# Attention tiles of 8 rows and 16 pixels instead of 4 rows and 32, with x fetched once more for them

## Chip, cores and metric

The kernel runs on one core of a Trainium2 chip. The metric is the device time of one execution in microseconds: the median of the runs.

## What is computed

x has the shape (4, 256, 64, 64), float32. The first layer makes 49 logits for each pixel by a dilated 7x7 convolution and a 1x1 convolution, takes the softmax of them, and uses it to weight the 49 dilated neighbours of the pixel in all 256 channels. The second layer adds a gelu term with a state vector and normalises over the channels.

```python
k = conv(x, w1, padding 6, dilation 2) + b1          # 256 -> 128 channels, 7x7
k = conv(k, w2) + b2                                 # 128 -> 49, 1x1
attn = softmax(k, axis=1)
shifts = [xp[:, :, 2*u:2*u+64, 2*v:2*v+64] for u in range(7) for v in range(7)]
x = einsum('bkchw,bkhw->bchw', shifts, attn)
y = gelu(yc.T[None, :, None, :] + x * D)             # yc: scan over 64 steps
out = layernorm over channels of (x + y), times ln_w, plus ln_b
```

## The kernel before

Because of the dilation, rows and columns of one parity never meet the others. The kernel works in 8 units: batch (4) times the parity of the rows (2). A unit has 32 rows; the two parities of the columns, called w, stay side by side, each 32 pixels wide. The channels are two halves h of 128 partitions.

In each unit `conv(n, ...)` (line 457) computes the logits of unit n on TensorE, in 49 steps of 20 matmuls, from row combinations that GpSimd and VectorE make of the raw rows and that `v_high` (ScalarE) and `v_low` (VectorE) turn into two float16 parts. Between those steps TensorE does the attention of the unit before, m = n - 1. The order on each engine is written out by hand: `unit` on TensorE (line 586), on ScalarE (974), on VectorE (1522), on GpSimd (380). Engines meet by semaphores only, and each queue is served in order.

The attention of a unit goes like this. `turn_logits` transposes the logits, VectorE and ScalarE take the softmax, `turn_attention` transposes back, and ScalarE copies the result to AT (pixels on the free axis, the 49 taps on the partitions, three empty rows above and below). `spread` (516) then builds the band: for the 128 pixels of a tile (4 rows of 32) it selects with a shifted 0/1 matrix `sel`, column by column, the weight with which each input pixel of the tile goes into each output pixel around it. A call covers one of the 10 output rows of all 16 tiles: 32 matmuls of 16 columns into one PSUM bank, which `band_high` (ScalarE, 915) and `band_low` (VectorE, 1484) copy out as two float16 parts. `apply` (530) multiplies x by the band: a call y covers one half of the rows (q), one channel half (h), one column parity (w), and for each tile that reaches these rows three matmuls (high x high, low x high, high x low). The moving side is up to 10 rows of 32 pixels of the band; the weights are the 128 pixels x 128 channels of XT. XT is made by `turn_x` (571), which transposes the tiles' pixels out of the raw rows of the unit, and by `turned_x` (ScalarE, 895) and `turned_x_low` (VectorE, 1387).

After `apply`, `attended` (ScalarE, 920) copies the result to o, VectorE forms the gelu arguments (1492), ScalarE the gelu (930), VectorE the residual (1505), GpSimd the sums of the two channel halves (`sum_rows`, `sum_squares`), TensorE sums over the channels (`mean`, `variance`, 560 and 566), ScalarE spreads the means and takes the inverse deviation, VectorE centres and normalises, ScalarE applies scale and shift, and SP stores. x is loaded by SP into two buffers, raw0 and raw1, one unit ahead.

At the start the weights are combined and split, so unit 0 runs more slowly between that work; the last attention (m = 7) has no convolution beside it, has six PSUM banks for the spreads instead of two, and an order of its own.

## Time and profile before

| | |
|---|---|
| median of 3 runs | 812.79 us (812.68 to 813.52) |
| profiled execution | 813.03 us, of which the span is 810.9 us |
| TensorE busy | 758.2 us (93%), weight loads 448.2 us |
| VectorE busy | 677.6 us (84%) |
| ScalarE busy | 566.1 us (70%) |
| GpSimd busy | 191.0 us (24%) |
| DMA | 41.78 MB, 133598 packets, nearly all under 512 B |

All durations in the text come from the one profiled execution, of which the span is what the profile shows; 2.1 us lie around it. Of the span, 0 to 142 us are the start with unit 0 and the first attention's softmax, then come six like periods of 89.8 us up to 680.5 us, then the last two attentions. In the rows, L544 is line 544 of the kernel; PE is TensorE, PEld its weight loads, DVE VectorE, ACT ScalarE, POOL GpSimd, and ACTq or SPq the sequencer of an engine, where semaphore waits and DMA issues stand.

### The profile page before, as it was taken

The page shows a single profiled execution, that of the slowest core. Times are in us where ns is not written, and L with a number is a line of the kernel's source. Part 1 is how long each engine was busy: PE and PEld are TensorE (multiplying, and loading weights), DVE is VectorE, ACT ScalarE, POOL GpSimd, SP SyncE. Part 2 cuts the span into 40 slices and gives each one's busy share as a digit, 9 for nine tenths or more (in the row PEclk, how much of TensorE's full clock was granted, in tenths as well). Part 3 has the DMA queues.
Part 4 walks back from the last instruction along what each step waited for, and adds up shares of the span by engine and source line. Part 5 has one row for each costly group of instructions (what it writes and reads, how often), then busy time and mean ns, then how long its engine had stood idle before and what let it go on. Part 6 is the DMA issues. An engine that isn't in the chain of part 4 may idle for free.

```text
span 810.9 us, 27182 instructions
## 1 busy us (share of the span) xinstructions
PE 758.2 (93%) x12242; PEld 448.2 (55%) x12242; DVE 677.6 (84%) x867; ACT 566.1 (70%) x917; POOL 191.0 (24%) x102
## 2 busy tenths in 40 slices
PE   4969989999999999999999999999999999997994
PEld 1535545764567545664567545764567455754671
DVE  0898997989888988989888888998888888595765
ACT  2873545768786796678786787678786777568546
POOL 4114113114211341114301431115302421022011
PEclk9979999999999999999999999999999999999988
DMA  9460050001602035201702053201711020201104
GB/s 295 130 105 2 3 93 16 3 1 24 135 4 53 3 77 81 55 2 27 132 2 55 2 107 53 55 2 27 132 27 30 2 53 4 55 2 48 39 22 104
DMA packets 133598, 41.78 MB, mean 52 GB/s; under 512 B 133145, under 2 KB 133226, under 8 KB 133226
## 3 DMA queue, kind: packets, MB, share of 16 engines
q1 hardware_dynamic: 132248, 40.01, 22.2%
q8 instruction: 96, 1.57, 0.8%
q10 hardware_dynamic: 1234, 0.04, 0.1%
q14 instruction: 20, 0.16, 0.1%
HBM read 23.27 MB, written 16.78 MB: 49 GB/s over the span
## 4 chain that ended last, share of the span: by engine, by line
PE 42%; ACT 20%; DVE 17%; issue 5%; POOL 2%; DVEq 0%; ACTq 0%
PE cv L484 20%; PE wk L525 9%; PE wk L544 4%; ACT chs L903 4%; ACT V L860 4%; PE wk L583 3%; POOL chs L371 2%; PE ms L556 2%; DVE o L1507 2%; DVE V L1359 2%; DVE Z L1400 2%; ACT ms L953 1%; DVE XT L1390 1%; DVE chs L1459 1%; DVE o L1520 1%
## 5 line engine op out<-in xcount | busy, mean ns | idle before, releaser
L484 PE MATMUL cv<-V,W 128*32 128x496 f16 (+6 forms) x7840 | 428.2, 374 | 3.6 <-issue 1.9
L484 PEld LDWEIGHTS cv<-V,W 128*32 128x32 f16 (+1 forms) x7840 | 198.8, 96 | 201.4 <-issue 15.3
L860 ACT ACTIVATE V<-R,sc 128x1024 f16<-128x1024 f32 (+1 forms) x88 | 109.6, 1274 | 59.6 <-DVE R L1285 50.7
L346 POOL TENSOR_TENSOR R<-raw 128x1152 f32<-128x1152 f32 x32 | 93.1, 2909 | 205.6 <-DVE V L1359 102.8
L1359 DVE SCALAR_TENSOR_TENSOR V<-R,sc,V 128x1024 f16<-128x1024 f32 (+1 forms) x88 | 115.1, 1328 | 2.6 <-ACT V L860 2.6
L544 PE MATMUL wk<-band,XT 128*128 128x224 f16 (+1 forms) x900 | 97.3, 266 | 0.9
L544 PEld LDWEIGHTS wk<-band,XT 128*128 128x128 f16 x900 | 76.6, 98 | 24.6 <-ACT o L926 6.0
L525 PEld LDWEIGHTS wk<-AT,sel 128*128 128x128 f16 x2368 | 73.5, 100 | 15.0 <-issue 11.0
L525 PE MATMUL wk<-AT,sel 128*128 128x16 f16 x2368 | 77.8, 193 | 0.1
L371 POOL TENSOR_TENSOR chs<-o 128x1024 f32<-128x1024 f32 x14 | 45.1, 3223 | 132.1 <-DVE o L1507 123.1
L1285 DVE SCALAR_TENSOR_TENSOR R<-R 128x1024 f32<-128x1024 f32 (+1 forms) x56 | 70.3, 1287 | 0.0
L926 ACT ACTIVATE o<-wk,sc 128x512 f32<-128x512 f32 x56 | 40.0, 730 | 39.8 <-PE wk L544 39.7
L377 POOL TENSOR_TENSOR chs<-tg 128x1024 f32<-128x1024 f32 x14 | 33.9, 2422 | 120.0 <-ACT tg L939 120.0
L917 ACT CAST band<-wk 128x512 f16<-128x512 f32 x74 | 42.7, 587 | 25.4 <-PE wk L525 25.4
L1486 DVE TENSOR_TENSOR band<-wk,band 128x512 f16<-128x512 f32 x74 | 49.3, 688 | 11.3 <-ACT band L917 10.7
L897 ACT ACTIVATE XT<-wk,sc 128x512 f16<-128x512 f32 x64 | 42.8, 678 | 16.2 <-PE wk L583 15.9
L1390 DVE SCALAR_TENSOR_TENSOR XT<-wk,sc,XT 128x512 f16<-128x512 f32 x64 | 46.4, 745 | 6.6 <-ACT XT L897 6.6
L583 PEld LDWEIGHTS wk<-id,raw 128*128 128x128 f32 x256 | 34.9, 209 | 25.3 <-DVE XT L1390 10.5
L1501 DVE SCALAR_TENSOR_TENSOR tg<-o,dcol,yc 128x1024 f32<-128x1024 f32 x28 | 35.9, 1282 | 15.0 <-ACT o L926 15.0
L1520 DVE TENSOR_TENSOR o<-o,ms 128x1024 f32<-128x1024 f32 x28 | 32.9, 1217 | 15.6 <-ACT ms L956 15.6
L583 PE MATMUL wk<-id,raw 128*128 128x128 f32 x256 | 43.3, 306 | 2.0 <-DVE XT L1390 1.5
L1400 DVE SCALAR_TENSOR_TENSOR Z<-cv,sc,Z 128x512 f32<-128x512 f32 (+1 forms) x56 | 41.1, 746 | 3.2 <-ACT Z L871 1.2
(194 smaller groups left out, 916.9 us busy)
## 6 DMA issues: line engine op xcount, KB each, us to landing
raw<-in_x_dram SPq DMA_DIRECT2D x16, 1024.0 KB, 11.3
out_dram<-o SPq DMA_DIRECT2D x28, 512.0 KB, 4.5
w1raw<-in_L_conv_w_dram SPq DMA_DIRECT2D x2, 3136.0 KB, 16.8
out_dram<-o SPq DMA_DIRECT2D x8, 256.0 KB, 3.9
cm<-in_L_conv_Cmat_dram ACTq DMA_DIRECT2D x1, 32.0 KB, 8.3
dcol<-in_L_conv_D_dram ACTq DMA_DIRECT2D x2, 0.5 KB, 10.2
lnw<-in_L_conv_ln_w_dram ACTq DMA_DIRECT2D x2, 0.5 KB, 7.3
lnb<-in_L_conv_ln_b_dram ACTq DMA_DIRECT2D x2, 0.5 KB, 7.4
```

Of the source, the lines that this page charges most:

```text
L346: nc.gpsimd.tensor_tensor(R[buffer][:, :, :, :], rows_of(par, j + 2), rows_of(par, j), ALU.subtract).then_inc(pool_rows, 1)
L371: nc.gpsimd.tensor_tensor(chs[:, :], o[:, q, 0].rearrange("p r w -> p (r w)"), o[:, q, 1].rearrange("p r w -> p (r w)"), ALU.add).then_inc ...
L484: ins = pe.matmul(to.rearrange("p (w t c) -> p w t c", w=2, c=COLS)[:, :, :, c0:c1], W[:, ws, h * K7 + v, k0:k1], slot(n, a)[:, low, :, t0 ...
L525: ins = pe.matmul(spread_bank(m, r)[:, c * TILES:(c + 1) * TILES].rearrange("p (w j) -> p w j", w=2), sel[:, s, f:f + P], AT[:, :, r:r + 2 ...
L544: ins = pe.matmul(apply_bank(m, y)[:, (r0 - 16 * q) * COLS:(r1 - 16 * q) * COLS], XT[:, xl, 8 * w + j, h, :], band[:, bl, 8 * w + j, r0 - ...
L583: ins = pe.transpose(wk[:, g % 2, c:c + P], rows[:, w:4 * WIDTH:2], id32[:, :])
L860: nc.scalar.activation(v_array(n, a, 0), array(a), ACT.Identity, scale=sc[:, par, 3:4]).then_inc(vhi, 1)
L1285: nc.vector.scalar_tensor_tensor(out=part(*out), in0=part(*a), scalar=factor, in1=part(*b), op0=ALU.mult, op1=ALU.add).then_inc(row_made, 1)
L1359: nc.vector.scalar_tensor_tensor(out=v_flat(n, a, 1), in0=array_flat(a), scalar=sc[:, par, 3:4], in1=v_flat(n, a, 0), op0=ALU.mult, op1=AL ...
L1390: nc.vector.scalar_tensor_tensor(out=low, in0=wk[:, g % 2, :], scalar=sc[:, par, 3:4], in1=high, op0=ALU.mult, op1=ALU.subtract).then_inc( ...
L1400: nc.vector.scalar_tensor_tensor(out=out, in0=summed(n, s, p0, p1), scalar=sc[0:p1 - p0, par, scale:scale + 1], in1=other, op0=ALU.mult, o ...
L1486: nc.vector.tensor_tensor(band[:, 1, :, r, :], spread_bank(m, r).rearrange("p (c t) -> p t c", t=TILES), band[:, 0, :, r, :], ALU.subtract ...
```

## The change

The 128 pixels of a tile are now 8 rows of 16 pixels instead of 4 rows of 32: 4 x 2 tiles for each column parity, 16 in all as before. A tile reaches 14 output rows instead of 10, and 19 columns instead of 32 (16 and 3 beyond one edge; the other edge is that of the picture). The band is stored so: 8 groups of 14 rows, each of 2 x 19 columns. `spread` goes by columns of the tile instead of output rows. Eight calls handle two columns of both tiles each, with 28 matmuls; one call the columns 16 to 18 and -3 (56 matmuls), one the columns -2 and -1 (28 matmuls); the copies of the band take 448 elements, the last 224, instead of 512. `apply` has 18 matmuls a call instead of 15: for each of three tile rows and two tile columns three, over 11, 11 and 3 output rows of 19.

`turn_x` no longer reads the raw rows. A tile's 8 rows of 32 pixels (both column parities) are loaded again from DRAM, two DMAs (one for each h) of 128 KB for each pair of tiles, into three buffers in turn: the two halves of AT (free once the spreads of the unit are done) and a new one, xs. `fetch_rows` on ScalarE issues them, eight times in each unit: three behind the last `band_high`, and one each behind `turned_x` 0 to 4. The first three of unit 0 are issued by SP ahead of the second load of x. `turn_x` waits for its rows. The number and shape of the transposes, and of the copies after them, stay.

In unit 0 the `turn_x` calls stand later between the convolution steps, and `turned_x` 0 and 1 and their low parts on ScalarE and VectorE with them. `sel` has 13 shifted patterns instead of 7 in the same space, so GpSimd writes 26 selections instead of 14; of AT it clears only the six empty rows.

```diff
+TROWS, TCOLS = 8, 16
+XROWS, XTILES = ROWS // TROWS, COLS // TCOLS
+STAGES = XROWS * XTILES
+BROWS = TROWS + 2 * PAD
+BCOLS = TCOLS + PAD
+SPREAD = tuple(((c, None), (c + 1, None)) for c in range(0, TCOLS, 2))
+SPREAD += (((16, 0), (17, 0), (18, 0), (-3, 1)), ((-2, 1), (-1, 1)))
...
 def spread(m, r):
-                for c in range(COLS):
-                    s = c + 1 if c < PAD else c - COLS + 7 if c >= COLS - PAD else 0
-                    f = (BROWS - 1 - r) * COLS + COLS - 1 - c
-                    ins = pe.matmul(spread_bank(m, r)[:, c * TILES:(c + 1) * TILES].rearrange("p (w j) -> p w j", w=2),
-                                    sel[:, s, f:f + P],
-                                    AT[:, :, r:r + 29:4, c], start=True, stop=True)
+                for k, (c, edge) in enumerate(SPREAD[r]):
+                    v = 3 - c if c < PAD else c - 6 if c > TCOLS - PAD - 1 else 0
+                    for row in range(BROWS):
+                        f = v * SEL_STEP + (BROWS - 1 - row) * TCOLS + BCOLS - 1 - c
...
+                            attention = AT[:, :, row:last:TROWS, c:c + TCOLS + 1:TCOLS]
...
+                        ins = pe.matmul(to, sel[:, f:f + P], attention, start=True, stop=True)
 def apply(m, y):
-                for j in range(ROWS // 4):
-                    r0, r1 = max(4 * j - PAD, 16 * q), min(4 * j + 4 + PAD, 16 * q + 16)
+                for j in range(XROWS):
+                    r0, r1 = max(TROWS * j - PAD, 16 * q), min(TROWS * j + TROWS + PAD, 16 * q + 16)
...
+                    for e in range(XTILES):
+                        to = out_rows[:, r0 - 16 * q:r1 - 16 * q, (COLS - BCOLS) * e:(COLS - BCOLS) * e + BCOLS]
+                        for k, (xl, bl) in enumerate(((0, 0), (1, 0), (0, 1))):
+                            ins = pe.matmul(to, XT[:, xl, 2 * (XTILES * j + e) + w, h, :],
+                                            band[:, bl, XROWS * w + j, r0 - TROWS * j + PAD:r1 - TROWS * j + PAD,
+                                                 BCOLS * e:BCOLS * e + BCOLS],
 def turn_x(n, par, g, cold=False):
-                        rows = raw[par][:, h, PAD + 4 * j:PAD + 4 * j + 4, :].rearrange("p r w -> p (r w)")
-                        ins = pe.transpose(wk[:, g % 2, c:c + P], rows[:, w:4 * WIDTH:2], id32[:, :])
+                k = STAGES * n + g
+                pe.wait_ge(xs_in[k % 3], 32 * (k // 3) + 32)
...
+                        rows = stage(k)[:, h].rearrange("p r c -> p (r c)")
+                        ins = pe.transpose(wk[:, g % 2, c:c + P], rows[:, w:2 * P:2], id32[:, :])
...
+            def fetch_rows(n, g):
+                k = STAGES * n + g
+                if g < 3:
+                    act.wait_ge(sel_done, STEPS * n)
+                    act.wait_ge(xt_done, STAGES * n)
+                else:
+                    act.wait_ge(xt_done, k - 2)
+                for h in range(HALVES):
+                    act.dma_start(stage(k)[:, h], tile_rows(n, g, h)).then_inc(xs_in[k % 3], 16)
```

## Rows read from the trace of the kernel before

**Rows 1.** Busy time, one steady unit: length, each engine; clock, DMA share, GB/s.

```profile
231.30:321.08 89.78, 87.86 (x1504) 52.47 (x1508) 78.93 (x96) 68.22 (x111) 23.39 (x9) 1.00 0.24 49
```

**Rows 2.** TensorE's timeline: start, duration, instructions merged, idle before and its releaser.

```profile
281.00 1.08 PE L556 MATMUL ms<-chs,ones 128*64 128x512 f32 x4 [0.40 <-POOL chs L377]
...
289.03 1.08 PE L556 MATMUL ms<-chs,ones 128*64 128x512 f32 x4 [1.03 <-DVE o L1520]
```

**Rows 3.** Chain that ended last, 233 to 271 us: start, duration, engine, target, line.

```profile
233.44 2.04 PE wk L525 x64
...
250.39 3.22 PE cv L484 x60
253.61 3.15 PE wk L544 x30
...
256.88 0.02 ACTq L866
...
257.40 0.95 ACT V L860
...
263.95 2.37 DVE o L1507 x2
...
266.39 3.35 POOL chs L371
...
269.79 1.08 PE ms L556 x4
```

**Rows 4.** ScalarE's timeline, 250 to 283 us.

```profile
250.42 0.59 ACT L917 CAST band<-wk 128x512 f16<-128x512 f32 x1 [0.40 <-PE wk L525]
255.33 0.73 ACT L926 ACTIVATE o<-wk,sc 128x512 f32<-128x512 f32 x1 [4.32 <-PE wk L544]
...
280.15 0.69 ACT L897 ACTIVATE XT<-wk,sc 128x512 f16<-128x512 f32 x1 [1.74 <-PE wk L583]
280.86 1.28 ACT L948 ACT_TABLE_LOAD   x1
282.16 0.66 ACT L948 ACTIVATE ms<-ms,eps 128x512 f32<-128x512 f32 x1
```

**Rows 5.** DMA issues: two of ScalarE's sequencer; lines 309 and 303 with landing.

```profile
2.11 1.50 ACTq L1065 DMA_DIRECT2D dcol<-in_L_conv_D_dram  x2
...
6.68 0.96 ACTq L1073 DMA_DIRECT2D lnb<-in_L_conv_ln_b_dram  x2
...
L309 SPq DMA_DIRECT2D out_dram<-o x28: 372/372/1875, 199.6 to 768.4; - x28
...
DMA to landing us min/median/max: 3.8/4.5/6.3
...
L303 SPq DMA_DIRECT2D raw<-in_x_dram x14: 540/3075/6227, 44.9 to 571.0; - x14
...
DMA to landing us min/median/max: 7.0/10.8/14.0
```

**Rows 6.** Costliest groups: busy us, mean ns of one | idle before, releaser.

```profile
L917 ACT CAST band<-wk 128x512 f16<-128x512 f32 x74 | 42.7, 587 | 25.4 <-PE wk L525 25.4
L1486 DVE TENSOR_TENSOR band<-wk,band 128x512 f16<-128x512 f32 x74 | 49.3, 688 | 11.3 <-ACT band L917 10.7
```

**Rows 7.** Timelines of the start: two waits of VectorE, one of ScalarE.

```profile
67.31 1.28 DVE L1359 SCALAR_TENSOR_TENSOR V<-R,sc,V 128x1024 f16<-128x1024 f32 x1 [0.86 <-ACT V L860]
...
74.12 0.75 DVE L1400 SCALAR_TENSOR_TENSOR Z<-cv,sc,Z 32x512 f32<-32x512 f32 x1 [1.20 <-ACT Z L871]
...
99.32 1.92 ACT L891 ACTIVATE tg<-raw 128x2048 f32<-128x2048 f32 x1 [5.79 <-DVE W L1686]
```

**Rows 8.** Last unit: two pieces of the chain, then VectorE's timeline.

```profile
775.23 4.06 PE wk L544 x30
779.29 6.07 PE cv L544 x60
...
781.51 0.74 DVE L1905 SCALAR_TENSOR_TENSOR o<-wk,sc,tg 128x512 f32<-128x512 f32 x1
```

More of the change, by code:

```diff
@@ L33 @@
 LN_EPS = 1e-5
-SEL_TAPS = ((0, 7), (3, 7), (2, 7), (1, 7), (0, 6), (0, 5), (0, 4))
-SEL_AT = PAD * COLS + COLS - 1 - PAD
+SEL_TAPS = ((0, 7),) + tuple((v, 7) for v in range(1, 7)) + tuple((0, v) for v in range(6, 0, -1))
+SEL_AT = K7 * TCOLS + TCOLS - 1
+SEL_STEP = SEL_AT + (K7 - 1) * TCOLS + K7
+SEL_WIDTH = (len(SEL_TAPS) - 1) * SEL_STEP + 2 * SEL_AT + (K7 - 1) * TCOLS + K7
+SEL_DONE = 2 * len(SEL_TAPS) + 1
+SPREAD = tuple(((c, None), (c + 1, None)) for c in range(0, TCOLS, 2))
+SPREAD += (((16, 0), (17, 0), (18, 0), (-3, 1)), ((-2, 1), (-1, 1)))
+STEPS = len(SPREAD)
 ATT_SCALE = 4096.0
@@ L194, in conv_seq_kernel @@
         raw = (raw0, raw1)
+        stages = [AT[:, w, PAD:PAD + ROWS, :].rearrange("p r c -> p (r c)").bitcast(F32) for w in range(2)] + [xs[:, :]]
+        tile_rows = lambda n, g, h: xv[n // 2, n % 2, h][:, TROWS * (g // XTILES):TROWS * (g // XTILES) + TROWS,
+                                                         2 * TCOLS * (g % XTILES):2 * TCOLS * (g % XTILES) + 2 * TCOLS]
+        stage = lambda k: stages[k % 3].rearrange("p (h r c) -> p h r c", h=HALVES, r=TROWS)
         ms = ctx.enter_context(nc.psum_tensor("ms", [P, 2, BANK], F32))
@@ L202, in conv_seq_kernel, with band_step @@
         last_banks = [wk[:, 0, :], wk[:, 1, :]] + [cv[:, i, :] for i in range(4)]
+        spread_out = lambda m, s: spread_bank(m, s)[:, 0:2 * XROWS * BROWS * 4].rearrange(
+            "p (n e c) -> p n e c", e=2, c=2)
+        edge_out = lambda m, s: spread_bank(m, s)[:, 0:2 * XROWS * BROWS * len(SPREAD[s])].rearrange(
+            "p (n c) -> p n c", c=len(SPREAD[s]))
+        def band_step(low, s):
+            rows = band[:, low].rearrange("p n r x -> p (n r) x")
+            if s < TCOLS // 2:
+                return rows.rearrange("p n (y z) -> p n y z", z=2)[:, :, s:s + 12:11, :]
+            first = TCOLS if s == TCOLS // 2 else TCOLS + len(SPREAD[s - 1])
+            return rows[:, :, first:first + len(SPREAD[s])]
+        sum_of_step = lambda m, s: (spread_out if s < TCOLS // 2 else edge_out)(m, s)
         spread_bank = lambda m, r: last_banks[r % 6] if m == LAST else wk[:, r % 2, :]
@@ L323, in _ @@
             sp.wait_ge(s_gmax, HALVES * GROUPS)
+            for g in range(3):
+                for h in range(HALVES):
+                    sp.dma_start(stage(g)[:, h], tile_rows(0, g, h)).then_inc(xs_in[g], 16)
             load(1, 1, 0)
@@ L805, in _ @@
             keep_running(2)
-            for r in range(BROWS):
+            for r in range(STEPS):
                 spread(m, r)
@@ L916, in band_high @@
                 act.wait_ge(sel_done, 10 * m + r + 1)
-                nc.scalar.copy(band[:, 0, :, r, :],
-                               spread_bank(m, r).rearrange("p (c t) -> p t c", t=TILES)).then_inc(bhi, 1)
+                nc.scalar.copy(band_step(0, r), sum_of_step(m, r)).then_inc(bhi, 1)
             def attended(m, par, y):
@@ L1008, in unit @@
                 band_high(m, 9)
+                fetch_rows(n, 0)
+                fetch_rows(n, 1)
+                fetch_rows(n, 2)
                 attended(m, other, 0)
@@ L1036, in unit @@
                 turned_x(n, par, 4)
+                fetch_rows(n, 7)
                 spread_mean(m, 1)
@@ L1163, in _ @@
             weights_high(4, 8)
-            turned_x(0, 0, 0)
             v_high(0, 0, 4)
             v_high(0, 0, 5)
+            turned_x(0, 0, 0)
+            fetch_rows(0, 3)
             weights_high(8, 10)
+            sum_1(0, 0)
             turned_x(0, 0, 1)
-            sum_1(0, 0)
+            fetch_rows(0, 4)
             v_high(0, 0, 6)
@@ L1173, in _ @@
             turned_x(0, 0, 2)
+            fetch_rows(0, 5)
             v_high(0, 0, 9)
@@ L1176, in _ @@
             turned_x(0, 0, 3)
+            fetch_rows(0, 6)
             sum_2(0, 0)
@@ L1181, in _ @@
             turned_x(0, 0, 4)
+            fetch_rows(0, 7)
             turned_x(0, 0, 5)
@@ L1228, in _ @@
             scale_shift(m - 1, 1, 1)
-            for r in range(4, BROWS):
+            for r in range(4, STEPS):
                 band_high(m, r)
@@ L1748, in _ @@
             v_low(0, 0, 3)
-            turned_x_low(0, 0, 0)
             make_x2_minus(0)
@@ L1753, in _ @@
             weights_low(5, 6)
+            turned_x_low(0, 0, 0)
             make_y2_plus(0)
             v_low(0, 0, 5)
-            turned_x_low(0, 0, 1)
             logit_scales(0, 0)
@@ L1759, in _ @@
             make_y2_minus(0)
+            turned_x_low(0, 0, 1)
             weights_low(6, 7)
@@ L1860, in _ @@
             nc.vector.tensor_scalar(ds[:, :], dcol[:, :], scale_of_last, None, ALU.mult).then_inc(l_scale, 1)
-            for r in range(BROWS):
+            for r in range(STEPS):
                 band_low(m, r)
```

71 lines of the change are left out of this document (41 added, 30 removed).

## The prediction

> **What bounds the kernel now.** I read first the table of busy time by stretch, to see whether one engine carries the steady units. One unit is 89.78 us; TensorE is busy for 87.86 of them, VectorE for 78.93 and ScalarE for 68.22, at a granted clock of 1.00 [rows 1]. That invites a wrong conclusion: that whatever TensorE is spared comes off the time. So I read next TensorE's timeline for where it waits. It waits little, but where it does it is for the normalisation chain of the other engines: 0.40 us for GpSimd's sum of squares before `variance`, 1.03 us for VectorE's `normalise` before the second `mean` [rows 2]. Last I read the chain of waits piece by piece. From the turned attention to the end of `apply(m, 1)` at 256.76 it runs gapless on TensorE: convolution, spreads, two applies. From 256.76 to 269.79 it does not. It goes ScalarE (evacuations, `v_high`, table load, gelu), VectorE (two residuals in 2.37 us), GpSimd (`sum_rows`, 3.35 us), and only then the `mean` matmuls [rows 3]. TensorE fills the same 13.0 us with six applies (3.15 us a pair, 9.5 us) and three convolution steps (3.2 us): 12.7 us. The two are tied, so an apply made cheaper there shows up as a wait of TensorE. Behind the mean the same holds: VectorE works without a gap up to the squares, GpSimd's sum releases `variance`, ScalarE then runs without a gap through two table loads and the exponentials [rows 4].
>
> I call the stretches B (turned attention to the end of `apply(m, 1)`), C (to the first `mean`), D (to `variance(m, 0)`), E (to the second `mean`) and A (from the last `turn_x` to the next turned attention; softmax on VectorE and ScalarE, tied with 14 convolution steps).
>
> **Spread.** Before: 10 calls of 32 matmuls, 320 a unit. 64 of them take 2.04 us, 31.9 ns each for 16 columns: the pair with its weight load sets the price, not the columns [rows 3]. After: eight steps of 28, one of 56, one of 28, 308 a unit, of 16 or 8 columns. Saved: 12 x 31.9 ns = 0.38 us a unit, all in B. A strided PSUM target is new; I add nothing for it, since 16 columns are 7 ns of the 32.
>
> **Copies of the band.** 512 elements cost 587 ns on ScalarE and 688 ns on VectorE [rows 6]. After, nine of ten have 448 and one 224. In proportion VectorE's become 602 ns; unchanged they stay 688; writing pairs of two-byte elements could cost more, and no row shows that. I take about 0.63, nearest to the proportional end because most of such a row is per element. The gain, some 0.06 us a step, is not on the path in itself: it keeps VectorE just ahead of the spreads, which are now closer together.
>
> **Apply.** Before, a call has 15 matmuls over 37 rows of 32, 3 x 1184 = 3552 columns: 1.48 us at 2.4 GHz, and 3.15/2 = 1.575 measured, so 6.3 ns a matmul on top [rows 3]. After it has 18 matmuls over 25 rows of 19, twice: 2850 columns. Twelve have 209 columns: 12 x (87.1 + 6.3) = 1.12 us. Six have 57, which is 24 ns, less than the 31.9 that a pair costs in the spread: 6 x 31.9 = 0.19 us. Together 1.31, saved 0.26 a call (0.1 if rows of 19 read badly, 0.33 if the short ones pay nothing extra). A unit has eight calls, 2.1 us. Only the first two lie in B: 0.53 us on the path. The other six lie in C, where ScalarE's chain sets the end; their 1.6 us becomes a wait of TensorE before the first mean.
>
> The Trainium skill ("TensorE: Matmul & The Clock Gate", section "Wait — 56ns, not 53.3ns?") gives a floor near 25 ns for a small matmul and 2.5 ns beyond its columns. By that the six short ones would cost 26 ns each, not 31.9, and the two calls on the path 0.07 us less a unit, half a microsecond in all. The rows here show 6.3 and 31.9 ns with weight loads between, and the sum goes by them.
>
> **The row loads.** Each unit gains 8 `fetch_rows` of two DMAs, each 128 partitions x 8 pieces of 128 B. All but the first six are issued by ScalarE, in the middle of its compute queue. No DMA of the trace stands between compute of an engine, so two things must be bounded. First, the issue: two issues took 0.96 us (`lnb`) and 1.50 us (`dcol`) on ScalarE, and 0.372 each for stores of 2048 pieces on SP [rows 5]. I take 0.96 a fetch. Second, how much of it delays compute: between nothing and all. For nothing speaks one row: at 256.88 ScalarE's queue stands at line 866, the wait of `sum_2`, although `v_high(10)`, which comes ahead of it, starts only at 257.40 [rows 3]. The sequencer runs ahead of the engine, so an issue can hide under the instructions already handed over. I take the hidden end, and price each place:
> - Fetches 0 to 2 stand between the last band copy (250.42) and the first evacuation (255.33), where ScalarE is idle for 4.32 us [rows 4]. Six issues are 2.9 us: hidden, with 1 us to spare after the shift of B. At 1.50 a fetch the cover is just gone.
> - Fetch 3 lies before the wait for the residual; fetch 4 is issued under the first square and the copy of `turned_x(1)`; 6 and 7 under exponentials and copies handed over earlier. Nothing.
> - Fetch 5 stands behind `turned_x(2)`, for whose matmuls the sequencer waited until 280.15. Its 0.96 us sticks out over the 0.71 to the table load at 280.86, after which Ln follows at once at 282.16 [rows 4]: +0.25, with the fetch's waits +0.3 us a unit in E.
>
> `turn_x` gains a wait for the rows; behind it on TensorE stands the rest of the unit. The tightest is fetch 7, issued while ScalarE waits for the second mean, by about 289.03, and needed by `turn_x(7)` after that mean (1.08 us), `turn_x(5)` (0.7), four steps (4.3) and `turn_x(6)` (0.35) [rows 2, 3]: 6.4 us later. Stores of 2048 pieces land in 3.8 to 6.3 us, loads of 4096 in 7.0 to 14.0 [rows 5]. 1024 pieces are nearest to the former. No stall taken, up to 1 us possible.
>
> **Start.** SP issues six small DMAs (2.5 us) ahead of `load(1, 1, 0)`, whose rows nothing in this stretch waits for, and GpSimd makes 12 more selections before the first rows of x are there: both hidden. The two first `turn_x` move behind convolution steps. Up to the maximum of x VectorE has two waits of weight, 0.86 us at 67.31 and 1.20 us at 74.12 [rows 7]. `turned_x_low(0, 0, 0)` moves from before to behind the first, and (0, 0, 1) from before to behind the second; block 1 of the convolution, which ends the second, now holds one `turn_x` (0.68 us) more. So +0.68 and +0.66, and `bound(1, 1, 0)`, which waited for VectorE's last weights at 99.32 [rows 7], passes it on: +1.3 us (0 to 1.4).
>
> **Last unit.** The spreads save 0.38. The first apply runs partly at half clock and saves 0.4. A pair of applies takes 4.06 us at first, then four calls 6.07, 1.52 each; VectorE needs two copies a call like the one of 0.74, less some overlap, 1.42 [rows 8]. At 1.31 TensorE would wait for VectorE, so only 0.1 a call is gained, 0.6 in all. Sum -1.3 us (-0.5 to -2).
>
> **Sum.** A unit: -0.38 - 0.53 + 0.3 = -0.6 us. Seven units: -4.2. Start +1.3 and end -1.3 cancel. The profiled execution took 813.03 us (a span of 810.9 and 2.1 around it), so 808.8 for it; it stands 0.24 above the median of the runs, 812.79, and for that I predict 808.6. Bounds of the terms: B -0.3 to -1.0, E 0 to +0.5; start and end -2 to +0.9: 804 to 815.
>
> **Rivals.**
> 1. *ScalarE's issues are not hidden* (slower). If a DMA holds the engine as a computation does, fetch 4 delays the square and with it `variance`, fetch 5 is then level with it, and 6 and 7 delay the copies that release the last `turn_x` and the softmax: 3 x 0.96 = 2.9 us a unit in D and E, against 0.9 saved. 7 x 2.0 = +14: 827. For it: from 280.15 on one row of ScalarE begins where the last ends [rows 4]. Against it: the row at 256.88. It turns the sign once more than 0.9 us a unit sticks out, a third of the issue time. Half of it gives 817.
> 2. *TensorE's whole saving counts*: 2.5 x 7 + 2 = 19 us, 794. For it: 98% busy. Against it: the chain in C, tied within 0.3 us.
> 3. *Rows come late.* Landing as the raw loads do, 11 us, fetch 7 stalls TensorE for 4.5 us a unit, 6 and 5 less: +30 us, 840. For it speak the pieces half as long as those of x. The Trainium skill ("DMA: Bandwidth & Descriptors", "Specifications") asks for pieces of 512 B or more for full rate; the traffic here, 256 B, has the same fault already and fills a share of 0.24 [rows 1].
> 4. *It moves nothing measurable*: copies or starting order eat what B saves, 811.2 to 814.4.
>
> **How the numbers follow.** Forecast and its neighbourhood (804 to 811.2) 0.50; rival 2 or part of it 0.10; rival 4 0.12; rival 1 in full or part 0.22; rival 3 0.06. The forecast's own range is 804 to 811; since rival 1 is too likely to leave out, the range reaches to it: 803 to 827, leaving out rivals 2 and 3. A change of under 0.2% (1.6 us) can't be told from none here. Faster 0.60, same 0.12, slower 0.28.
>
> **What would show it.** Right: spread pairs near 1.79 us, apply pairs near 2.6, period 89.2, a new TensorE wait of 1.5 to 2 us at line 556 on GpSimd's `sum_rows`, ScalarE's DMA rows lying inside the time of its computations. Wrong: gaps of 0.9 us in ScalarE behind `turned_x` (rival 1), TensorE waiting at the transposes on a DMA (rival 3), band copies above 0.69 us, or a clock below 1.00 in the steady units because TensorE now idles and its matmuls are short.

## The result and the profile after

| | before | after |
|---|---|---|
| median of 5 runs | 812.79 us (812.60 to 813.78) | 809.60 us (807.29 to 811.15) |
| profiled execution, of it the span | 813.03, 810.9 us | 809.6, 807.6 us |
| TensorE, VectorE, ScalarE busy | 758.2, 677.6, 566.1 us | 746.6, 672.8, 562.8 us |
| DMA packets | 133598 | 266721 |

The ratio is 0.9951 (95% interval 0.9937 to 0.9965): 0.5% faster. TensorE is busy for 11.6 us less, and the span is 3.3 us shorter. A second profiled execution with new timing runs gave 0.9959 (0.9945 to 0.9973).

I cut each unit at four marks on TensorE's timeline: the start of the turned attention, the start of `apply(m, 0)`, the first mean, the second row of the mean's line (that is `variance(m, 0)`), the third (the second mean). I call the pieces B', C', D and E; the prediction's B ends two applies later than B', and its C begins there. Pieces of a like unit (in us):

| | B' | C' | D | E | rest | mean period |
|---|---|---|---|---|---|---|
| before | 23.30 | 16.25 | 11.21 | 8.02 | 31.0 | 89.83 |
| after | 22.90 | 15.93 | 11.21 | 8.37 | 31.0 | 89.57 |

So TensorE's stretch gives 0.39 in the spreads and 0.32 in the first two applies, E gives 0.35 back, and nothing else moves: -0.36 a unit. The mean period (first to seventh turned attention, divided by six) shows less, since in unit 1 E is 9.10, where fetch 5 took 1.69 us. Unit 7, the last with a convolution beside it, gains 0.9 (C' goes from 15.89 to 15.01 there), so the sum over all seven comes to 2.5 all the same. In the whole span: -2.5 us from the first turned attention to the second mean of the last full unit (597.4 to 594.9), +2.7 ahead of it (140.48 to 143.16), -3.5 behind it (73.0 to 69.6).

One like unit of after, columns as in [rows 1]:

```profile
233.33:322.74 89.41, 86.35 (x1512) 52.29 (x1513) 78.39 (x95) 67.86 (x110) 23.32 (x9) 1.00 0.41 73
```

TensorE works 1.5 us less in it than in [rows 1], but the unit is only 0.37 shorter. The DMA share went from 0.24 to 0.41 and stalled no transposition. The chain that ended last in the same unit (start, duration, what), which answers to [rows 3]:

```profile
236.54 1.86 PE wk L575 x56
...
250.78 2.31 PE wk L575 x84
...
253.17 0.37 ACTq L957
...
256.74 1.64 ACTq L957
...
258.48 0.71 ACT o L989
...
266.33 2.37 DVE o L1583 x2
...
268.77 3.36 POOL chs L411
...
272.17 1.08 PE ms L606 x4
```

A piece is new (ACTq, ScalarE's sequencer): the six DMA issues of fetches 0 to 2 (line 957) run from 253.17 to 258.38, and the first evacuation starts behind them. That they stand in the chain doesn't say that they cost time: TensorE's applies 0 and 1 end at the same time, and sp_fetch below tells the two apart. The rest of the chain in C is as before. TensorE's timeline (idle time before the row and its releaser in brackets), which answers to [rows 2]:

```profile
268.74 2.90 PE L596 MATMUL wk<-band,XT 128*128 128x57 f16 x36
272.17 1.08 PE L606 MATMUL ms<-chs,ones 128*64 128x512 f32 x4 [0.53 <-POOL chs L411]
...
283.38 1.08 PE L606 MATMUL ms<-chs,ones 128*64 128x512 f32 x4 [0.41 <-POOL chs L417]
...
291.75 1.08 PE L606 MATMUL ms<-chs,ones 128*64 128x512 f32 x4 [1.37 <-DVE o L1596]
```

The new wait of 0.53 us for GpSimd's sum is what TensorE was spared in C. The wait at the second mean grew from 1.03 to 1.37, and ScalarE's timeline shows from where, which answers to [rows 4]:

```profile
278.21 1.06 ACT L1002 ACTIVATE tg<-o 128x1024 f32<-128x1024 f32 x1 [1.63 <-DVE o L1583]
278.22 1.01 ACTq L957 DMA_DIRECT2D xs<-in_x_dram  x2
...
282.54 0.69 ACT L961 ACTIVATE XT<-wk,sc 128x512 f16<-128x512 f32 x1 [1.74 <-PE wk L634]
282.54 1.01 ACTq L957 DMA_DIRECT2D AT<-in_x_dram  x2
283.58 1.28 ACT L1011 ACT_TABLE_LOAD   x1 [0.36 <-issue]
```

Fetch 4 is issued inside the square (278.22 in 278.21 to 279.27): hidden. Fetch 5 starts with `turned_x(2)`, lasts 1.01 us against 0.69, and the table load waits 0.36 us for the sequencer. Copies of the band, which answer to [rows 6], and all fetches issued by ScalarE (ns min/median/max of one, then landing):

```profile
L981 ACT CAST band<-wk 128x448 f16<-128x448 f32 x74 | 40.2, 557 | 23.9 <-PE wk L575 23.3
L1562 DVE TENSOR_TENSOR band<-wk,band 128x448 f16<-128x448 f32 x74 | 42.7, 600 | 11.0 <-ACT band L981 10.6
```

```profile
L957 ACTq DMA_DIRECT2D AT<-in_x_dram x82: 373/601/1640, 67.4 to 737.2; - x82
L957 ACTq DMA_DIRECT2D xs<-in_x_dram x40: 373/601/2109, 85.5 to 735.4; - x40
...
DMA to landing us min/median/max: 2.4/3.0/4.4
```

At the start, TensorE's first convolution steps before and after, then VectorE's and ScalarE's waits that answer to [rows 7]:

```profile
56.01 8.15 PE L484 MATMUL cv<-V,W 128*32 128x512 f16 x120 [1.85 <-issue]
```

```profile
56.81 8.61 PE L526 MATMUL cv<-V,W 128*32 128x512 f16 x120 [4.09 <-issue]
...
76.19 0.75 DVE L1476 SCALAR_TENSOR_TENSOR Z<-cv,sc,Z 32x512 f32<-32x512 f32 x1 [1.88 <-ACT Z L924]
...
102.05 1.91 ACT L944 ACTIVATE tg<-raw 128x2048 f32<-128x2048 f32 x1 [5.76 <-DVE W L1762]
```

In the last unit the clock differs: busy time and clock of the same ten microseconds, before and after, then the first pair of applies of after, which answers to [rows 8] (4.06 us):

```profile
767.50:777.50 10.00, 9.56 (x179) 7.13 (x176) 4.58 (x8) 5.51 (x8) 0.00 (x0) 0.52 0.41 105
```

```profile
767.50:777.50 10.00, 10.00 (x232) 9.24 (x229) 5.94 (x11) 6.41 (x11) 0.00 (x0) 1.00 0.48 108
...
773.67 2.89 PE L596 MATMUL wk<-band,XT 128*128 128x209 f16 x36
```

Before, TensorE ran there at 1.2 GHz (granted clock 0.52), in and behind the last spreads; after, at 2.4 (1.00). TensorE's six matmuls between the last spreads and the first apply, before and after:

```profile
772.67 2.56 PE L790 MATMUL ms<-W,id 128*128 128x480 f16 x6
```

```profile
772.46 1.38 PE L843 MATMUL ms<-W,id 128*128 128x480 f16 x6
```

### The profile page after: what moved, and what is told of

Its sections match the earlier page's. It is cut to its first block, busy times and chain, and to the rows that moved or that the text cites. A ratio compares the mean times of both kernels' runs of the same rounds, so it can differ in the third digit from the quotient of the medians.

```text
span 807.6 us, 27610 instructions
## 1 busy us (share of the span) xinstructions
PE 746.6 (92%) x12338; PEld 446.8 (55%) x12338; DVE 672.8 (83%) x867; ACT 562.8 (70%) x917; POOL 194.6 (24%) x115
## 2 busy tenths in 40 slices
DMA packets 266721, 58.60 MB, mean 73 GB/s; under 512 B 266265, under 2 KB 266346, under 8 KB 266346
## 4 chain that ended last, share of the span: by engine, by line
PE 35%; ACT 22%; DVE 16%; issue 9%; POOL 3%; ACTq 2%; DVEq 0%; POOLq 0%
PE cv L526 18%; PE wk L575 7%; ACT V L913 5%; ACT chs L967 4%; DVE V L1435 3%; PE wk L596 3%; PE wk L634 3%; POOL chs L411 2%; PE ms L606 2%; ACTq L957 2%; DVE o L1583 2%; ACT ms L1016 1%; DVE Z L1476 1%; DVE XT L1466 1%; DVE chs L1535 1%
## 5 line engine op out<-in xcount | busy, mean ns | idle before, releaser
L386 POOL TENSOR_TENSOR R<-raw 128x1152 f32<-128x1152 f32 x32 | 95.2, 2976 | 201.5 <-DVE V L1435 102.4
L596 PE MATMUL wk<-band,XT 128*128 128x209 f16 (+1 forms) x1080 | 87.7, 238 | 3.3 <-ACT o L989 3.0
L596 PEld LDWEIGHTS wk<-band,XT 128*128 128x128 f16 x1080 | 78.7, 97 | 15.0 <-ACT o L989 8.5
L575 PEld LDWEIGHTS wk<-AT,sel 128*128 128x128 f16 x2268 | 69.6, 100 | 15.0 <-issue 8.6
L575 PE MATMUL wk<-AT,sel 128*128 128x16 f16 (+1 forms) x2268 | 73.9, 190 | 0.1
L1361 DVE SCALAR_TENSOR_TENSOR R<-R 128x1024 f32<-128x1024 f32 (+1 forms) x56 | 68.6, 1257 | 0.0
L981 ACT CAST band<-wk 128x448 f16<-128x448 f32 x74 | 40.2, 557 | 23.9 <-PE wk L575 23.3
L1562 DVE TENSOR_TENSOR band<-wk,band 128x448 f16<-128x448 f32 x74 | 42.7, 600 | 11.0 <-ACT band L981 10.6
L606 PE MATMUL ms<-chs,ones 128*64 128x512 f32 x112 | 31.1, 633 | 18.2 <-DVE o L1596 9.9
L1356 DVE TENSOR_TENSOR R<-R 128x1024 f32<-128x1024 f32 x32 | 43.9, 1371 | 0.1
```

The source lines that it names most:

```text
L386: nc.gpsimd.tensor_tensor(R[buffer][:, :, :, :], rows_of(par, j + 2), rows_of(par, j), ALU.subtract).then_inc(pool_rows, 1)
L575: ins = pe.matmul(to, sel[:, f:f + P], attention, start=True, stop=True)
L596: ins = pe.matmul(to, XT[:, xl, 2 * (XTILES * j + e) + w, h, :], band[:, bl, XROWS * w + j, r0 - TROWS * j + PAD:r1 - TROWS * j + PAD, BCO ...
L606: ins = pe.matmul(ms[LO * e:LO * e + LO, 0, :], ones[:, 0:LO], chs[:, e * BANK:(e + 1) * BANK], tile_position=(0, LO * e), skip_group_chec ...
L1356: nc.vector.tensor_tensor(part(*out), part(*a), part(*b), op).then_inc(row_made, 1)
L1361: nc.vector.scalar_tensor_tensor(out=part(*out), in0=part(*a), scalar=factor, in1=part(*b), op0=ALU.mult, op1=ALU.add).then_inc(row_made, 1)
```

## The experiments

All times are against runs of the kernel before on the same chip; the pieces are those of units 2, 4 and 6 (1 to 7 counted by their turned attention) where nothing else is said. Two theories ran through them. Mine: only B and what sticks out of ScalarE's issues count. The rival of the prediction: TensorE's whole saving counts. The first four runs asked this.

**cut_b**, apply 0 and 1 made cheaper still:

```diff
+                drop = m < LAST and y < 2
...
-                    if r0 >= r1:
+                    if r0 >= r1 or (drop and r1 - r0 <= 3):
```

> The changed kernel, but apply calls 0 and 1 of units 1 to 7 leave out the six matmuls over three output rows (a part of the result is missing). By the pair of applies of the changed kernel (2.85 us for 36 matmuls, 12 x 93.4 ns a call for the long ones) the six cost 0.31 us a call, so TensorE is spared 0.61 us a unit in stretch B. Theory A (the fetches 0 to 2, whose issue ends 5.0 us after the last band copy, are now level with the end of apply 0 and 1): the first two evacuations can come only 0.1 to 0.3 us earlier, the gap of ScalarE behind the issue of the sixth DMA becomes the bound; -0.2 us a unit, -1.5 us in all, about 808. Theory B (stretch B is TensorE's alone): -0.6 a unit, -4.3 in all, about 805.3.

Measured: 809.12 us, ratio 0.9948 (0.9931 to 0.9965). C' is 15.61 in units 1 to 4, so -0.32 us a unit there, a little more than theory A said. But not for its reason, as sp_cut_b shows below: there the issues are gone, and the gain is the same 0.34. What was wrong is the price of the short matmuls: 12 of them are worth 0.33 us, 28 ns each, not 51.

**cut_c**, the other six calls made cheaper (the same diff with `y >= 2`):

> The changed kernel, but apply calls 2 to 7 of units 1 to 7 leave out the six matmuls over three output rows (a part of the result is missing). TensorE is spared 6 x 0.31 = 1.8 us a unit in stretch C. Theory of the stretches: C is set by ScalarE, VectorE and GpSimd, the time stays within 0.3 us a unit (808 to 810), and TensorE's wait for the sum of rows before the first mean grows by about 1.4 us, to 2 us. Rival (TensorE's whole time counts, since it is busy for 97% of a unit): -1.8 a unit, -12.8 in all, about 797.

Measured: 808.23 us, ratio 0.9941 (0.9926 to 0.9956). C' 15.90 instead of 15.93. TensorE's timeline:

```profile
446.72 2.56 PE L597 MATMUL wk<-band,XT 128*128 128x209 f16 x24
...
450.32 1.08 PE L607 MATMUL ms<-chs,ones 128*64 128x512 f32 x4 [1.03 <-POOL chs L411]
```

A pair of calls is 2.56 us for 24 long matmuls against 2.90 for 36, so 28 ns for a short one again, and TensorE was spared 6 x 0.17 = 1.0 us a unit. The time of the unit did not move; the wait for GpSimd's sum went from 0.53 to 1.03, the rest into the waits for the evacuations. This settles it for units 1 to 6: what TensorE is spared in C counts for nothing. Only in unit 7 did it count in part (C' 15.01 to 14.80). The wait was expected to grow by 1.4 us and grew by 0.5, since the short matmuls cost 28 ns and not 51.

**sp_fetch**, the issues taken off ScalarE:

```diff
-                fetch_rows(n, 0)
-                fetch_rows(n, 1)
-                fetch_rows(n, 2)
                 attended(m, other, 0)
...
+                    sp.dma_start(stage(k)[:, h], tile_rows(n, g, h)).then_inc(xs_in[k % 3], 16)
...
             for n in range(1, UNITS):
-                store(n, n % 2, (n - 1) // 2, 0)
+                for g in range(7):
+                    fetch_rows(n, g)
+                store(n, n % 2, (n - 1) // 2, 0, (0,))
+                fetch_rows(n, 7)
+                store(n, n % 2, (n - 1) // 2, 0, (1,))
```

> The changed kernel, but all row fetches are issued by SyncE instead of ScalarE, in the same order, fetch 7 between the two stores of the first half of a unit. Theory A (the issues on ScalarE cost what sticks out: 0.41 us at fetch 5 ahead of the table load, and nothing or little at fetches 0 to 2, which are level with the applies): the gap ahead of the table load of the first inverse deviation is gone, -0.4 us a unit, -3 us in all, about 806.6. Rival (the issues are hidden): within 0.5 us of 809.6. Second rival (a transfer issued later on SyncE, behind a store, stalls the transposes): slower, with waits of TensorE on a DMA at the last transposes.

Measured: 808.55 us, ratio 0.9954 (0.9933 to 0.9975). E is 8.02, that of before, and the table load follows its copy without the 0.36 us. ScalarE's timeline, then TensorE's:

```profile
282.92 1.28 ACT L1016 ACT_TABLE_LOAD   x1
```

```profile
291.09 1.08 PE L622 MATMUL ms<-chs,ones 128*64 128x512 f32 x4 [1.03 <-DVE o L1588]
...
298.28 0.72 PE L650 MATMUL wk<-id,xs 128*128 128x128 f32 x4 [0.45 <-DMA xs<-in_x_dram]
```

C' stays 15.93, so in most units the burst of six cost nothing. The price of fetch 5 is shown: 0.35 us a unit. In the timed runs the gain doesn't show (0.9954 against 0.9951, where 7 x 0.35 us would be 0.3%): behind the store, fetch 7 came late for its transposes in some units (0.45 us here), and the first 140 us were 0.8 longer in this execution.

**sp_cut_b**, both:

> Both edits: the fetches issued by SyncE, and apply calls 0 and 1 without their six matmuls over three output rows (a part of the result is missing). Theory A (ScalarE's six issues and TensorE's end of stretch B are level): with both gone the stretch gives its full 0.6 us a unit beyond the kernel with the fetches on SyncE, -1.0 a unit together, -7 in all, about 802.5; the sum of the two single edits would be only -4.5. Theory B (stretch B is TensorE's alone, the issues cost 0.4 in E): the two edits add up, the same -7, but then the cut alone had given -4.3.

Measured: 805.34 us, ratio 0.9902 (0.9887 to 0.9918). B' 22.92, C' 15.58, D 11.22, E 8.01. The two edits add up piece by piece (-0.35 in C', -0.36 in E): theory B in form, with 0.34 where it had 0.6. The profile of cut_b shows what became of its 2.3 us in that execution: in units 5 and 6 the six issues took 5.24 and 5.63 us (C' 15.92 and 16.26); one fetch 5 took 1.72 us (E 9.08), and behind it TensorE, after a wait of 2.08 us, ran at a lower clock for a while, so that the rest of unit 5 took 32.48 us instead of 31.0; in unit 4 fetches 6 and 7 took 3.25 us, and TensorE waited 0.57 us at a transpose (rest 31.65). The expected 802.5 was missed by as much as the short matmuls had been priced too high.

The next four asked whether the time that TensorE now waits in C can be used, and what stands against it.

**move_step** and **sp_move_step**, one convolution step from B to C, with the fetches on ScalarE and on SyncE:

```diff
-                conv(n, 27, 30)
+                conv(n, 27, 29)
                 apply(m, 0)
...
-                conv(n, 30, 33)
+                conv(n, 29, 33)
```

> The changed kernel, with one convolution step (1.07 us) moved from ahead of apply 0 to behind apply 5, so from stretch B into stretch C, where TensorE waits about 1.1 us in three places. Fetches stay on ScalarE. Apply 0 then ends 1.6 us before the sixth issue does. Theory A (the six issues in a row, 5.0 us, are ScalarE's bound as soon as the applies come earlier): B -1.07, but from apply 0 to the first mean +0.7 to +0.9; net -0.2 to -0.4 us a unit, -2 us in all. Theory B (issues hidden): net -1.0 a unit, -7 in all. Theory C (TensorE has no slack in C): 0.

> The same step moved, and the row fetches issued by SyncE. Theory A: B -1.07 us, C as it is or +0.1 (TensorE's waits there are used up), E -0.35 as in the kernel with the fetches on SyncE: -1.3 us a unit against the changed kernel, -9 in all, about 800.5. Theory C (no slack in C): -0.35 a unit, about 807.

Measured: move_step 812.74 us, ratio 0.9998 (0.9983 to 1.0012); sp_move_step 803.72 us, ratio 0.9882 (0.9861 to 0.9903). B' is 21.9 in both. With SyncE C' is 16.36 in units 1 to 6, +0.43; D is 0.37 shorter and E 0.37 longer, since TensorE reaches `variance` with the sum already there. So C had room for 0.6 of the step's 1.07 us and not for 1.0, which is most of why 803.7 was measured and not 800.5. With ScalarE C' goes from 16.58 to 17.88, and it follows the length of the six issues:

| move_step, unit | 1 | 2 | 3 | 4 | 5 | 6 |
|---|---|---|---|---|---|---|
| six issues, us | 4.75 | 5.81 | 4.93 | 4.49 | 5.47 | 4.61 |
| C' less 16.36 | 0.47 | 1.52 | 0.66 | 0.22 | 1.19 | 0.35 |

The difference of the two rows is 4.26 to 4.29 us in all six: this is the cover that the issues have when apply 0 comes a step earlier. In the changed kernel it is one step (1.07) longer, 5.3 us, and the seven bursts there took 4.54 to 5.35: used up, not exceeded. In start_order (below) one burst took 5.63 us, and C' of that unit is 16.26: exceeded by 0.3. ScalarE's timeline in unit 2 of move_step, then TensorE's:

```profile
253.58 1.41 ACTq L957 DMA_DIRECT2D AT<-in_x_dram  x2
255.08 1.33 ACTq L957 DMA_DIRECT2D xs<-in_x_dram  x2
256.51 2.88 ACTq L957 DMA_DIRECT2D AT<-in_x_dram  x2
259.49 1.32 ACT L989 ACTIVATE o<-wk,sc 128x512 f32<-128x512 f32 x2 [5.59 <-PE wk L596]
```

```profile
260.25 4.47 PE L596 MATMUL wk<-band,XT 128*128 128x209 f16 x54 [1.73 <-ACT o L989]
```

The bracket of ScalarE's row names TensorE; but that apply had ended at about 257, and the row above shows the queue in the issues until 259.39. Theory A was right and too mild: -0.2 expected, +0.1 on average, and 3 us slower than the changed kernel, part of it clock (below).

**start_order**, the start as before:

```diff
+            turn_x(0, 0, 0, cold=True)
+            turn_x(0, 0, 1, cold=True)
             conv(0, 0, 6, cold=True)
-            turn_x(0, 0, 0, cold=True)
-            conv(0, 6, 10, cold=True)
-            turn_x(0, 0, 1, cold=True)
-            conv(0, 10, 16, cold=True)
             turn_x(0, 0, 2, cold=True)
...
```

> The changed kernel with the starting order of the kernel before: the first two transposes of x ahead of the first convolution step (in the 4.1 us in which TensorE waits there), the third behind step 6, the fourth behind step 14, and the copies turned_x and turned_x_low 0 and 1 on ScalarE and VectorE where they stood. From the start of the first convolution step to the first turned attention the kernel before takes 84.5 us, the changed one 86.35, and four experiments so far 86.2 to 86.5. Theory (the two transposes in the path of block 1, two copies of VectorE moved behind its waits, and 0.45 us of lower clock in the first steps): back to 84.5 to 85.0, -1.4 to -1.9 us. Rival (the rows, issued at 45.7 us and later, land too late for the early place): TensorE waits there on the DMA and nothing is won.

Measured: 809.30 us, ratio 0.9948 (0.9928 to 0.9968). From the first convolution step (58.65) to the first turned attention (143.72) 85.07 us, 1.28 less than the 86.35 of the changed kernel, and no wait for the rows. TensorE's timeline:

```profile
54.35 1.19 PE L634 MATMUL wk<-id,AT 128*128 128x128 f32 x8 [0.47 <-issue]
58.65 8.79 PE L526 MATMUL cv<-V,W 128*32 128x512 f16 x120 [3.12 <-issue]
```

The transposes fit ahead of the steps. The stretch is just outside the 84.5 to 85.0 that were expected; in the two kernels with the old tiling measured below it took 84.4 and 85.1 us with this starting order, so it scatters by more than half a microsecond. In the timed median the gain doesn't show.

**combo**, all of it: fetches on SyncE, start as before, one step to C and one to E:

```diff
-                conv(n, 27, 30)
+                conv(n, 27, 28)
...
-                conv(n, 30, 33)
+                conv(n, 28, 32)
...
-                conv(n, 33, 40)
+                conv(n, 32, 39)
...
-                conv(n, 40, 45)
+                conv(n, 39, 45)
```

> Fetches on SyncE, the starting order of the kernel before, one step moved from B to C, and one more from B to E, where TensorE waits 1.0 us for VectorE's normalise. Theory: B -2.14 us, less up to 0.6 where the copies of the last band steps or VectorE's work ahead of the first gelu argument come late; C +0.1; E +0.05; with E's 0.35 and the start's 1.6: -1.9 us a unit against the changed kernel, 809.6 - 13.5 - 1.6 = 794.5 (792 to 798). Rival (VectorE, which has 1.6 us of wait left ahead of the first gelu argument, becomes the bound of B at once): one step only, 799.

Measured: 795.36 us, ratio 0.9775 (0.9758 to 0.9792), 2.2% faster than before, the best of all and near the expected 794.5. B' 20.81, so the full 2.1 us, C' 16.36, D 10.84, E 8.39, mean period 87.56. TensorE's timeline, and the unit:

```profile
264.52 1.08 PE L622 MATMUL ms<-chs,ones 128*64 128x512 f32 x4
...
275.36 1.08 PE L622 MATMUL ms<-chs,ones 128*64 128x512 f32 x4
...
283.75 1.08 PE L622 MATMUL ms<-chs,ones 128*64 128x512 f32 x4 [0.31 <-DVE o L1586]
```

```profile
227.35:315.32 87.97, 86.20 (x1512) 52.23 (x1513) 78.47 (x95) 67.98 (x110) 23.32 (x9) 1.00 0.40 74
```

The waits at the first two are gone and 0.31 us is left at the third. TensorE does the same work as in the changed kernel (86.2 us), in 1.4 us less; this unit is the longest of the six (its rest took 31.6 us), the mean period is 2.0 shorter. The start took 84.56 us from the first step, 1.8 less than in the changed kernel.

**before_e1** and **before_c1e1**, the old tiling with the step order of these (conv 27 to 29, 32, 39, 45; and 27 to 28, 32, 39, 45):

> The kernel before (old tiling), with one convolution step moved from stretch B to stretch E, where TensorE waits 1.03 us for VectorE's normalise; C and D hold as many steps as before. Theory (B is TensorE's, E is VectorE's and ScalarE's): B -1.07, E +0.05 us, -1.0 a unit, -7 in all, about 806. Rival (a step later is a sum of the convolution later, and the logits of VectorE wait for it): 810 or more.

> The kernel before, with one step moved from B to E and one from B to C, the order of the combined kernel. Theory: in C the old applies leave TensorE only 0.3 us (12.7 of 13.0), so the step moved there costs 0.8 of its 1.07: -1.3 us a unit against the kernel before, about 804. The new tiling in the same order of steps (795.4, of which about nothing is the start, since both have the same) is then 8 to 9 us faster: that, and not 3, is what the tiling spares TensorE (0.39 in the spreads and 8 x 0.155 in the applies, 1.6 us a unit) less what it can't use. Rival (the combined kernel's gain is all from the order): within 2 us of 795.4.

Measured: before_e1 805.87 us, ratio 0.9909 (0.9891 to 0.9927); before_c1e1 808.47 us, ratio 0.9935 (0.9919 to 0.9952). The step into E gives 1.0 us a unit, as expected. The second was expected to give 0.3 more (804) and gives nothing: against before_e1 C' is 0.86 longer (17.14) and B' only 0.75 shorter, since the last copies of the band are now late, as TensorE's timeline says. That is 0.1 us a unit, so most of the 2.6 us between the two medians lies elsewhere; in the profiles 0.9 us of it is the start.

```profile
252.75 3.50 PE L544 MATMUL wk<-band,XT 128*128 128x224 f16 x33 [0.27 <-DVE band L1486]
```

So the better of the two orders tried with the old tiling gives 805.9, and the new one with the order of combo 795.4, 1.3% less (0.9775 / 0.9909 = 0.9865). Of these 10.5 us some 9 lie in the seven units (a mean period of 88.84 against 87.56). In the same order of steps the medians differ by 13.1 us, where 8 to 9 were expected; by the period (88.91 against 87.56) it is 9.5 in seven units, the rest lies at the start and the end, part of it clock. So some 9 us is what the tiling is worth once TensorE's time counts; in the change as made 3 us of it showed. Other orders of the old tiling, one step into C alone among them, were not tried.

**halved_fetches**, twice as many issues for the same bytes, fetches 0 to 2 on SyncE so that only the single places count:

```diff
                 for h in range(HALVES):
-                    act.dma_start(stage(k)[:, h], tile_rows(n, g, h)).then_inc(xs_in[k % 3], 16)
+                    for part in (slice(0, 4), slice(4, 8)):
+                        act.dma_start(stage(k)[:, h, part], tile_rows(n, g, h)[:, part]).then_inc(xs_in[k % 3], 16)
...
```

> The changed kernel, with fetches 0 to 2 of a unit issued by SyncE, and each fetch cut into four DMAs of 64 KB instead of two of 128 KB (pieces of 128 B as before, the same bytes), so ScalarE issues 20 DMAs a unit in D and E where it issued 10 there. Theory A (an issue takes its time on ScalarE's queue whatever its size, and what sticks out over the instruction handed over before it delays the rest): fetch 5 takes 2.0 us against the 0.7 of the copy ahead of it, so E is 1.0 us longer than the changed kernel's 8.36, fetch 4 sticks out 0.3 in D: +1.3 us a unit, +9 in all, about 818. Theory B (the issue goes by the number of pieces): as the changed kernel, 809. Theory C (issues are hidden): 806 to 809, E at 8.0.

Measured: 833.84 us, ratio 1.0242 (1.0211 to 1.0272). Four issues of half the size take 2.05 us where two took 1.01: the cost goes by the issue, not by the pieces (theory A). ScalarE idles 1.40 us ahead of the table load instead of 0.36, and 0.53 ahead of the second square; D 11.75 and E 8.87 in the milder units, +1.04 together. But the loss is 24 us, not 9. The rest is longer in all six units, by 0.8 to 1.5 us, together 6.6 us. In unit 2 it is clock: behind a wait of TensorE of 1.87 us the granted clock was 0.72 and then 0.65 for 5 us. And in three units D is 14.2 to 14.6. GpSimd's sum of squares in unit 3 with VectorE's rows beside it, then GpSimd's sum and VectorE's row in unit 2:

```profile
376.90 4.66 POOL L430 TENSOR_TENSOR chs<-tg 128x1024 f32<-128x1024 f32 x1 [9.88 <-ACT tg L1016]
```

```profile
376.95 0.68 DVE L1496 SCALAR_TENSOR_TENSOR Z<-ev,Z 128x512 f32<-128x512 f32 x1
377.55 0.68 DVE L1496 SCALAR_TENSOR_TENSOR Z<-Z 128x512 f32<-128x512 f32 x1
378.15 1.22 DVE L1367 TENSOR_TENSOR R<-R 128x1024 f32<-128x1024 f32 x1
```

```profile
284.42 2.35 POOL L430 TENSOR_TENSOR chs<-tg 128x1024 f32<-128x1024 f32 x1 [9.39 <-ACT tg L1016]
```

```profile
284.59 2.73 DVE L1496 SCALAR_TENSOR_TENSOR Z<-ev,Z 128x512 f32<-128x512 f32 x1
```

An operation of 2.35 us takes 4.66, or VectorE's of 0.68 takes 2.73. In unit 3 VectorE's three operations take their usual time and GpSimd's ends 2.3 us behind the last of them; in unit 2 GpSimd's takes its usual time and VectorE's ends 0.6 us behind it. So one of the two stands while the other works. The square came half a microsecond later, and GpSimd's sum with it, which in unit 3 fell behind VectorE's work instead of ahead of it; TensorE then waited 3.75 us for the sum.

**after_again**, the changed kernel a second time:

> The changed kernel once more, for a second profiled execution beside these. Expected: B 22.9, C 15.95, D 11.21, E 8.37 in most units, as in the first; other values only where a fetch on ScalarE takes 1.7 us or more instead of 1.0 (unit 1 in the first profile, E 9.10); 86.3 us from the first convolution step to the first turned attention. The last 70 us and the first 40 may differ by up to 2 us each with the stretches in which TensorE runs at half clock.

Measured: 810.38 us, ratio 0.9959 (0.9945 to 0.9973). The pieces B' to E are those of the first, to 0.02 us in units 2, 4 and 6, and E of unit 1 is 9.32, where fetch 5 took 1.91 us. From the first step to the first turned attention it took 86.24 us, and the last stretch 69.55 us, as in the first profile (86.35 and 69.57).

## Why the prediction was right, and where not

The time was predicted as 808.6 and measured as 809.6. That is closer than the working deserved: three terms were off, and their errors cancel, which is luck.

| us | predicted | measured |
|---|---|---|
| seven units | -4.2 | -2.5 |
| start | +1.3 | +2.7 |
| last unit | -1.3 | -3.5 |

- **What bounds the kernel.** Right, and shown by cut_c. The applies of C were spared 0.16 us each and later another 0.17, without effect in units 1 to 6. Rival 2 (794) is out for this order of steps. combo comes to its number (795.4), but not by the tiling alone: the order of steps gives the old tiling 7 us by itself (before_e1).
- **Spread.** 0.38 predicted, 0.39 measured (B'), but by two errors that cancel. 56 matmuls of 16 columns take 1.83 to 1.86 us, 33.0 ns each and not 31.9 (1.79 us were named as the sign): with 224 of them that loses 0.25 us a unit. The 84 of 8 columns take 2.31 us, 27.5 ns each, which gains 0.37. So "the pair with its weight load sets the price, not the columns" is not quite so, and the strided target, for which I added nothing, may be the 1.1 ns; no run separates it.
- **Apply.** This step failed by size: 0.26 us a call predicted, 0.155 measured. The error is in the long matmuls, not the short ones. A call now takes 1.575 - 0.155 = 1.42 us, six short ones are 0.17 of it (cut_c), so a long one takes about 104 ns, where I had put 87.1 + 6.3. The old rows of 32 gave the 6.3; eleven rows of 19 cost 17 on top of their columns. Whether that is the short rows of the band, those of the target, or both, no run separates. My end of the range, "0.1 if rows of 19 read badly", was the right neighbourhood. The short ones were too dear in my sum (31.9; measured 28), and its other end, 0.33, should be 0.31 by its own terms. The Trainium skill ("TensorE: Matmul & The Clock Gate", section "Wait — 56ns, not 53.3ns?") has a floor near 25 ns for a small matmul and 2.5 ns on top of the columns of a long one. The first fits the 28 ns; by an estimate from the second a long one would cost 90 ns, and the rows show 104.
- **The wait in C.** 1.5 to 2 us at the mean was predicted. 0.53 is at the mean and 0.4 at the applies, which wait for the evacuations; the sum is smaller because the applies were spared less.
- **Fetches 0 to 2.** "Six issues are 2.9 us: hidden, with 1 us to spare" is wrong in size: the six took 4.5 to 5.4 us, 0.75 to 0.9 each in a row, where a pair takes 1.01. The cover was 5.3 us and not the 4.32 of the gap in [rows 4]: the first issue starts while the last copy runs, and the first evacuation may come some 0.8 us late, since the second waits for its apply anyway. So the cost was next to nothing, and by luck: in move_step, with less cover, all that was longer counted in full.
- **Fetch 5.** +0.3 predicted, +0.35 measured and shown by sp_fetch. What was not foreseen is its scatter: now and then a pair takes 1.7 to 1.9 us, and E is 9.1 to 9.3 instead of 8.37.
- **The other fetches.** Hidden as said in the changed kernel; the rows landed in 2.4 to 4.4 us against 4.5 taken and 6.4 allowed. Rival 3 is out: no row of TensorE waits on a DMA from 140 us on. Rival 1 was right in kind and an eighth of its size here (0.35 of 2.9 us a unit); in halved_fetches more of it comes true (D and E 1.04 us longer in the milder units).
- **Band copies.** 0.60 us on VectorE, the proportional end (0.602) of what was bounded; I had taken 0.63.
- **Start.** The path from the first step on lost 1.9 us, 1.3 predicted. start_order gives 1.3 of it back. Most of the rest is clock: in the six first steps the granted clock was 0.74 (0.73 in start_order) against 0.79 before, and they took 8.6 to 8.8 us instead of 8.15; ahead of them TensorE had idled 4.09 and 3.12 us instead of 1.85. A further 0.8 us lay ahead of that and is not the change: eight of TensorE's matmuls at 27 us took 3.15 us at a granted clock of 0.53 where before they took 1.86 at 1.00. They took 3.0 to 3.3 us in eleven of the fourteen profiles, both others with the old tiling among them, and 1.85 or 1.86 in those of the kernel before, sp_cut_b and combo. So the start shown for before and for combo is flattered by about a microsecond.
- **Last unit.** -3.5 instead of -1.3. In all three profiles with the old tiling the six matmuls between the last spreads and the first apply took 2.56 us at 1.2 GHz (granted clock 0.50); with the new one they took 1.38 us at 2.4 GHz in eight of eleven profiles, and 2.35 to 2.44 us in the others. By the distance to the next row the six went from 2.36 to 1.21 us and the first pair of applies behind them from 4.09 to 2.73: together 2.5 us, of which my sum had 0.4. Earlier in the same stretch the new one lost some: at 747 us its granted clock was 0.51 for 2 us, where before it was 1.00. The clock was not in my sum: I took the half clock of [rows 8] as given. Why the old spreads bring it down and the new ones mostly don't is open.

## What to carry to other kernels

A saving counts only in the stretch in which its engine is the last to finish; elsewhere it becomes a wait, and the wait can be turned into time by moving work of the same engine out of the stretch that it bounds. Here that, with the issues taken off ScalarE and the start put back, was worth 14 us on top of the 3 of the change itself; one step moved in the old kernel was worth 7 without any new tiling. Before that, look for what has grown into the gap: here DMA issues in a compute queue cost nothing until they were the length of their cover, and from there on all that they were longer.

## What the runs showed of the hardware that I had not expected

- DMA issues of 128 KB took 0.37 and 0.60 us of ScalarE's queue as a pair (1.01 with what lies between), but 4.5 to 5.8 us for six in a row; those of half the size took the same each (2.05 us for four). SyncE's bursts of six were as long (4.5 to 6.1 us).
- GpSimd and VectorE shut each other out in halved_fetches: 2.35 us became 4.66, or 0.68 became 2.73. The Trainium skill ("SBUF — State Buffer", section "SBUF: two separate sides") says that the port pair that they share is an exclusive lock held for the whole instruction. These rows agree that one stands while the other works; GpSimd stood through three instructions of VectorE (0.68, 0.68 and 1.22 us).
- A wait of TensorE of some 2 us can be followed by half clock, or not. TensorE's timeline of start_order and of after_again at the same place:

```profile
203.30 1.95 PE L606 MATMUL ms<-chs,ones 128*64 128x512 f32 x4 [2.20 <-DVE o L1594]
```

```profile
202.25 1.08 PE L606 MATMUL ms<-chs,ones 128*64 128x512 f32 x4 [2.31 <-DVE o L1596]
```

The first ran at 1.2 GHz (granted clock 0.57 from 203 to 207 us), the second at 2.4 (1.00), and the rest of the first one's unit took 32.5 us instead of 31.0. With what sticks out of a long fetch 5 this may be most of the scatter between executions of the changed kernel (807.3 to 811.2); only two of them were profiled (809.6 and 809.3), so that is a guess.
